# Attention scores in two pairs of PSUM banks, one exponential over each pair

## What is computed

```python
q = _conv(query, Wq[idx], 'SAME').reshape(n, HEADS, HC, -1)
k = _conv(token, Wk[idx], 'VALID').reshape(n, HEADS, HC, -1)
v = _conv(token, Wv[idx], 'VALID').reshape(n, HEADS, HC, -1)
w = jax.nn.softmax(jnp.einsum('nhcq,nhcd->nhqd', q, k), axis=-1)
a = jnp.einsum('nhcd,nhqd->nhcq', v, w).reshape(n, CA, hh, ww)
```

## Time and profile before

| what | us |
|---|---|
| median of 3 runs | 377.89 |
| lowest and highest | 376.87, 380.81 |
| the profiled execution, its time | 378.51 |
| its span, first to last instruction | 376.5 |

### The profile page before, as it was taken

One profiled execution on the slowest core, in us unless ns is written; L12 is line 12 of the kernel. 1 busy time (PEld: TensorE's weight loads), 2 busy tenths in 40 slices (PEclk: granted clock), 3 DMA queues, 4 the chain that ended last, 5 costly groups with the idle time before them and its releaser, 6 DMA issues.

```text
span 376.5 us, 5797 instructions
## 1 busy us (share of the span) xinstructions
PE 317.9 (84%) x2186; PEld 109.5 (29%) x2186; DVE 230.0 (61%) x494; ACT 173.3 (46%) x334; POOL 38.9 (10%) x36
## 2 busy tenths in 40 slices
PE   5499655688998553999999999999999899885994
PEld 1133111232343111323332323323333222332931
DVE  5970054744836650468778687878776321579944
ACT  2100000002416443987879787897978787300000
POOL 5000600400000000001010000101010012505100
PEclk9989968999989865999999999999999999999798
DMA  2799995000157953230210303000000000000001
GB/s 85 163 196 211 190 200 162 0 3 0 38 166 147 124 109 125 84 113 2 60 55 1 113 3 113 2 1 3 0 1 2 1 3 0 2 0 1 3 2 56
DMA packets 6867, 23.89 MB, mean 63 GB/s; under 512 B 1272, under 2 KB 2040, under 8 KB 5912
## 3 DMA queue, kind: packets, MB, share of 16 engines
q1 hardware_dynamic: 6840, 23.53, 26.0%
HBM read 11.59 MB, written 2.37 MB: 37 GB/s over the span
## 4 chain that ended last, share of the span: by engine, by line
PE 48%; DVE 9%; issue 4%; ACT 2%; DVEq 0%; ACTq 0%
PE ps L1179 14%; PE ps L1161 14%; PE ps L1138 11%; DVE arena_a L463 3%; PE ps L1291 2%; ACT arena_b L678 2%; PE ps L1184 2%; PE ps L1234 1%; PE ps L1251 1%; DVE arena_a L966 1%; PE ps L1007 1%; PE ps L1299 1%; DVE arena_b L978 1%; DVE arena_a L990 1%; PE ps L1242 1%
## 5 line engine op out<-in xcount | busy, mean ns | idle before, releaser
L678 ACT ACTIVATE arena_b<-ps 128x512 f32<-128x512 f32 x232 | 125.2, 607 | 37.6 <-PE ps L1161 36.9
L1161 PE MATMUL ps<-arena_a 128*128 128x512 bf16 x224 | 85.0, 389 | 10.1 <-issue 9.5
L1138 PE MATMUL ps<-arena_a 128*128 128x450 bf16 x256 | 87.4, 371 | 6.5 <-issue 4.3
L890 DVE TENSOR_REDUCE mx<-ps 128x1 f32<-128x450 f32 x120 | 69.3, 618 | 6.5 <-PE ps L1138 4.8
L885 DVE CUSTOM_DVE_ANT_0 sums<-ps,relus 128x450 bf16<-128x450 f32 x68 | 41.4, 626 | 44.3 <-PE ps L1138 34.9
L1179 PE MATMUL ps<-arena_b,vt 128*32 128x512 f32 x448 | 59.7, 605 | 0.7 <-ACT arena_b L678 0.7
L1161 PEld LDWEIGHTS ps<-arena_a 128*128 128x128 bf16 x224 | 21.7, 98 | 80.6 <-ACT arena_b L678 50.4
L686 ACT ACTIVATE relus<-ps 128x450 f32<-128x450 f32 x68 | 37.5, 554 | 10.5 <-PE ps L1138 10.4
L1007 PE MATMUL ps<-zeros 128*128 128x512 bf16 x115 | 30.4, 406 | 7.7 <-DMA xa<-x 3.5
L1138 PEld LDWEIGHTS ps<-arena_a 128*128 128x128 bf16 x256 | 24.0, 100 | 39.9 <-issue 11.3
L640 ACT ACTIVATE arena_b<-ps 96x386 f32<-96x386 f32 x3 | 1.5, 490 | 63.9 <-PE ps L1056 63.8
(11 more groups left out here) (130 smaller groups left out, 244.2 us busy)
## 6 DMA issues: line engine op xcount, KB each, us to landing
arena_b<-arena_a SPq DMA_DIRECT2D x12, 578.0 KB, 10.3
arena_b<-wmodes SPq DMA_DIRECT2D x4, 1024.0 KB, 4.9
arena_a<-k_scratch SPq DMA_DIRECT2D x3, 516.8 KB
arena_b<-arena_a SPq DMA_DIRECT2D x4, 306.0 KB, 5.7
arena_a<-q_scratch SPq DMA_DIRECT2D x3, 384.0 KB
arena_b<-arena_a SPq DMA_DIRECT2D x4, 272.0 KB, 5.0
k_scratch<-arena_b SPq DMA_DIRECT2D x3, 344.5 KB, 3.7
cst<-consts SPq DMA_DIRECT2D x1, 1029.0 KB, 11.7
```

Source lines behind the costliest of these rows:

```text
L678: nc.scalar.activation(probs[:, n % PRING, :], ps[:, SCORE_RING[n % len(SCORE_RING)], :], ACT.Exp).then_inc(expd, 1)
L890: nc.vector.tensor_reduce(mx[:, a, e:e + 1], bank, AX.X, ALU.max).then_inc(max_read, 1)
L1138: mm(ps[:, block_bank(i), 0:KHALF], qst[:, e, g, qt * P:(qt + 1) * P], kst[:, g, at:at + KHALF], start=True, stop=True).then_inc(max_score ...
L1161: last = mm(ps[:, bank, :], kst[:, g, t * P:(t + 1) * P], qst[:, e, g, :], start=True, stop=True)
```

## The change

The eight banks are dealt out anew: banks 0 and 1, and 2 and 3, are two pairs for scores, banks 4, 5 and 6 are for max blocks, bank 7 is the only one for output sums. A full step now has two groups instead of four tiles: a group is the score tiles of two heads, in the two banks of a pair, and ScalarE takes one exponential of 1024 columns over both. The last keys still make one tile of 512 columns. A half so has 15 groups (`EXP_GROUPS`) and the whole attention 112 exponentials of 1024 and 8 of 512 columns. Group n waits for the exponential of group n-2. The ring of probabilities is the same memory as four slots of 1024.

The plan keeps its 4.15 blocks a step, but hands them out after each group, and `values` moves behind the second group and its blocks. The first `values` of every half but the first waits until the output sums of the half before have been transposed. The gates and output banks are renumbered, the prologue's max blocks run over seven banks instead of six, and one `keep_clock` uses bank 3 instead of 6.

```diff
-EXP_UNITS = HEADS * DT + 1
+EXP_GROUPS = 2 * DT + 1
 PRING = 8
+GROUP_SLOTS = PRING // 2
-SCORE_RING = (0, 1, 2)
-MAX_RING = (3, 4, 5)
-O_RING = (6, 7)
+SCORE_RING = (0, 2)
+MAX_RING = (4, 5, 6)
+O_BANK = 7
@@ attention_plan
         for t in range(DT + 1):
-            units = HEADS if t < DT else 1
+            units = 2 if t < DT else 1
             due += BLOCKS_PER_STEP * (1.0 if t < DT else 0.6)
             taken = 0
             for h in range(units):
-                plan.append(("score", s * EXP_UNITS + t * HEADS + h))
+                plan.append(("score", s * EXP_GROUPS + 2 * t + h))
                 k = int(due * (h + 1) / units + 1e-6)
                 take(k - taken)
                 taken = max(taken, k)
-                if prev and h == min(2, units - 1):
+                if prev and h == units - 1:
                     plan.append(("values", *prev))
@@ block_bank
-            ring = SCORE_RING + MAX_RING if i < prologue else MAX_RING
-            return ring[i % len(ring)]
+            return i % 7 if i < prologue else MAX_RING[i % len(MAX_RING)]
@@ ScalarE
+                    width = HALF if n % EXP_GROUPS == 2 * DT else 2 * HALF
+                    at = 2 * HALF * (n % GROUP_SLOTS)
                     act.wait_ge(scored, n + 1)
-                    if n >= PRING:
-                        old_half, old = divmod(n - PRING, EXP_UNITS)
-                        act.wait_ge(pv_done, old_half * (DT + 1) + old // HEADS + 1)
-                    nc.scalar.activation(probs[:, n % PRING, :], ps[:, SCORE_RING[n % len(SCORE_RING)], :], ACT.Exp).then_inc(expd, 1)
+                    if n >= GROUP_SLOTS:
+                        old_half, old = divmod(n - GROUP_SLOTS, EXP_GROUPS)
+                        act.wait_ge(pv_done, old_half * (DT + 1) + old // 2 + 1)
+                    nc.scalar.activation(probs_row[:, at:at + width], banks(SCORE_RING[n % 2])[:, 0:width], ACT.Exp
+                                         ).then_inc(expd, 1)
@@ score_tile
-                if n >= len(SCORE_RING):
-                    pe.wait_ge(expd, n - len(SCORE_RING) + 1)
+                if n >= 2:
+                    pe.wait_ge(expd, n - 1)
-                    t, h = divmod(i, HEADS)
-                    g = b * HEADS + h
-                    last = mm(ps[:, bank, :], kst[:, g, t * P:(t + 1) * P], qst[:, e, g, :],
-                              start=True, stop=True)
+                    t, pair = divmod(i, 2)
+                    for k in range(2):
+                        g = b * HEADS + 2 * pair + k
+                        last = mm(ps[:, bank + k, :], kst[:, g, t * P:(t + 1) * P], qst[:, e, g, :],
+                                  start=True, stop=True)
@@ values
-                if t == 0 and half >= len(O_RING):
-                    pe.wait_ge(o_read, half - len(O_RING) + 1)
+                if t == 0 and half >= 1:
+                    pe.wait_ge(o_read, half)
-                    pe.wait_ge(expd, n0 + HEADS)
+                    pe.wait_ge(expd, n0 + 2)
```

## The result

The changed kernel takes 390.28 us in the median (389.22 to 391.45, four runs) against 378.07 beside it, a ratio of 1.0313 (95% interval 1.0249 to 1.0378): 3.1% slower. The forecast was 391 us.

A forecast was written before the change was run, and what follows sets the result against it. TensorE was taken to bound the kernel; stalls of +2.5, +7.9, +2, +3.5 and +0.7, less 2.1 and 1.5, made +13.0 us, so 391 us on the 377.9 median. The range ran from 381 to 399.

The forecast's parts named there:

- TensorE's saturation: In steps with blocks, TensorE gives the pace: 2.73 us a step with nothing in it but work.
- The faster rival: Waits of scores for exponentials are real time that fewer handshakes would save, giving 372 us; chance 0.10.
- Block 1 plain: Steps whose first max block is a plain maximum: block 4 stalls 0.07 us, some 36 steps, +2.5 us.
- Block 1 a diff block: Relu queues behind the wide exponential, so block 4 stalls 0.71 us; 11 steps, +7.9 us.
- Fifth block: Five full steps have one more block, which needs block 2's bank: about 0.4 us each, +2 us.
- VectorE's transposes: Transposing a half's sums and back delays block 4 about 0.3 us, twice in each of six halves: +3.5 us.
- case 3: A diff block second, third or fourth in a step: its bank is wanted only after the values, so no cost.
- The stalls of before: The earlier kernel's 0.30 us of stalls a half, contained in the other terms, go off: -2.1 us.
- The last turn: It already waits 1.30 us for the split of the maxima; values no longer lie ahead of it: +0.7 us.
- The end without blocks: Steps after the max blocks run out fall from 2.47 to 2.08 us; four such steps, -1.5 us.
- The single output bank: Rival: a half's first values wait for the previous half's transpose, about 1 us in seven halves, 399 us; chance 0.16.
- A gap that repeats on the engine that should be saturated: Sign of too few PSUM buffers; if the forecast holds, the repeating gap is ahead of block 4.

The follow-up runs named there:

- e2: The changed kernel with a block handed out after every score tile again, same banks and wide exponentials; 380.36 us, ratio 1.0093 to the kernel before.
- e8: The kernel before with the changed order, four max banks instead of three and one output bank instead of two; 379.93 us, ratio 1.0048.
- e1: The changed kernel, but ScalarE takes a diff block's Relu directly behind a score group ahead of that group's exponential; 381.83 us, ratio 1.0131 to the kernel before.
- e4: The kernel before with one bank of output sums instead of two, all else unchanged; 377.91 us, ratio 1.0028.
- e3: The kernel before with its banks and narrow exponentials, and only the order of the changed one; 388.74 us, ratio 1.0325.
- e5: The changed kernel with each group's exponential issued as two of 512 columns, one behind the other; 391.49 us, ratio 1.0336 to the kernel before.

## Why the prediction was right, and where its terms were not

The mechanism was right: the order of the list left 1.00 us between block 1 and block 4, and a Relu behind an exponential made that a stall of 0.72 us. The closeness of the total is in part luck, as the terms below show.

**What bounds it.** TensorE's saturation held: where e2 takes the stalls away a step is 2.73 us, and at no point less while it has four blocks. The faster rival, that the waits for exponentials were real time, falls: e8 has even more of them (45.6 us) at nearly the time of before.

**Block 1 plain: 0.07 us a step, +2.5 us.** Measured 0.08, +2.9 over the 36 steps from V 0.0 to V 6.3 that don't start with a diff block.

**Block 1 a diff block: 0.71 us, 11 steps, +7.9 us.** Measured 0.72 in the steps that have nothing else in them, but in nine steps, +6.5. This was the term that decided. The list of steps was right; that steps 0 and 1 of half 0 run at half clock, right behind the prologue, was overlooked. In e1 the way from the first score to V 0.0 is only 0.2 us shorter than in the changed kernel.

**Fifth block: about 0.4 us.** Right in kind. The fifth blocks added 0.53, 0.64 and 0.76 us to their steps, of which 0.19 is the block's own work: 0.34 to 0.57 of stall. The costliest stand behind a first diff block; here block 5 of such a step, from the timeline of the changed kernel, waits for block 2, which VectorE could only read after the Relu:

```profile
213.88 0.36 PE L1142 MATMUL ps<-arena_a 128*128 128x450 bf16 x1 [0.55 <-ACT relus L690]
213.96 0.63 DVE L889 CUSTOM_DVE_ANT_0 sums<-ps,relus 128x450 bf16<-128x450 f32 x1 [2.16 <-PE ps L1142]
...
214.65 0.36 PE L1142 MATMUL ps<-arena_a 128*128 128x450 bf16 x1 [0.40 <-DVE mx L889]
```

**VectorE's transposes: +3.5 us, right in sum and wrong in its working.** I had priced two events of 0.3 us in each of six halves. Transposing back costs nothing: the steps that hold it are 2.81 us in four of six halves. What the transpose of the sums costs is in the passage from V s.6 to the first values of the next half. Its work is 5.20 us (the shortest passage in e1 and e2 is 5.21). Less that work, 0.08 for a plain step, 0.72 for a first diff block and 0.19 for a fifth block's work, the six passages have 0.7, 0.8, 0.3, 0.0, 1.5 and 0.3 us left, 3.6 in all. This holds everything that is not counted elsewhere, a fifth block's stall among it, and no run takes the transpose out by itself. By the timelines it is cheap where nothing else is late, and nothing where both steps are held by a Relu anyhow. It is dear where a partner is late. After half 4, a Relu at 266.93 holds its partner on VectorE to 267.61, the transpose stands in front of the next read, and a block waits for 1.03 us beyond TensorE's own work:

```profile
268.17 0.71 DVE L911 STREAM_TRANSPOSE ot<-ps 128x512 f32<-128x512 f32 x1
...
269.70 0.36 PE L1142 MATMUL ps<-arena_a 128*128 128x450 bf16 x1 [1.03 <-DVE mx L894]
```

That passage took 7.05 us, 1.39 over the best, a fifth block among it. The late Relu is that of a third block, for which case 3 of the prediction has "Nothing"; in e1, where it comes earlier, the passage is 0.83 us shorter. So case 3 holds for the block's own bank and not for what stands behind its partner on VectorE.

**The stalls of before: -2.1, measured -3.4.** Counted in the same way, the kernel before has 3.4 us of stall from V 0.0 to V 6.3; over half of it lies in each half's last interval, V s.5 to V s.6, and is gone in the new order.

**The stretch with blocks in sum.** My terms (2.5 + 7.9 + 2 + 3.5 - 2.1) make +13.8 us; measured +12.4. Term by term the trace has about 2.9 + 6.5 + 2.4 + 3.6 - 3.4, and 0.4 in small delays.

**The last turn: +0.7, measured +0.8.** It waits for 2.13 us instead of the 1.30 of the earlier trace rows.

```profile
305.29 0.22 PE L1148 MATMUL ps<-ident_b,mparts 128*48 128x128 bf16 x1 [2.13 <-DVE mparts L873]
```

**The end without blocks: -1.5 us.** The size is about right, the working is not. In half 7 it is -1.24, of which 0.21 is the score that this interval has less, so -1.0; in half 6 it is about -0.3, which is the table's +0.31 with the turn's 0.8 taken out and the missing block's 0.19 put back. I had steps of 2.08 us; they are 2.27 and 2.35 against 2.40 and 2.47:

```profile
320.05 1.07 PE L1185 MATMUL ps<-arena_b,vt 128*32 128x512 f32 x8
321.05 0.60 PE L1167 MATMUL ps<-arena_a 128*128 128x512 bf16 x2
321.86 0.61 PE L1167 MATMUL ps<-arena_a 128*128 128x512 bf16 x2 [0.21 <-ACT arena_b L681]
322.40 1.06 PE L1185 MATMUL ps<-arena_b,vt 128*32 128x512 f32 x8
```

ScalarE came into this step behind by the gates' and cell's work (it runs from 319.34 to 323.64 without a pause), so it, and not TensorE's 1.95, still holds the second group. That a longer stretch would reach the rhythm I had worked out is not shown.

**The total.** The terms added up to +13.0 us. The two traces differ by 10.7, of which -1.05 is the earlier first score and no part of the change; the medians differ by 12.2. So 391 against 390.28 looks better than the sum was: its terms were 1.4 us high in the stretch with blocks, and the medians lie further apart than the traces.

**The single output bank.** As rival it had 0.16 and would have given 399 us. e4 prices it at 0.2 us a half at most, in the order of before; in the changed kernel it does not bind. The rule of the Trainium skill (Perfetto Trace Analysis, Matmuls) on rotating matmul groups through banks holds here for the max blocks, where a fourth bank takes the ratio from 1.0325 (e3) to 1.0048 (e8), and is worth next to nothing for the output sums. A gap that repeats on the engine that should be saturated, which the Trainium skill (the same page, Optimization Strategy) gives as a possible sign of too few buffers, is what the changed trace shows ahead of block 4.

## What to carry to other kernels

Where one engine is full, an order written by hand is a set of distances between each producer and the reuse of its buffer: a change that moves a long item (here 1 us of values) out of the middle of a step shortens all distances that ran across it. The merged exponentials were not what cost: with the same order and narrow ones the step still took 3.30 us (e3), and with a block after every score and wide ones it took 2.73 (e2). So when a merge comes with a new order, test the two apart, and look for what now stands behind the long item in its engine's queue and who waits for that.

Price such a change by walking the new list on the clock of one step, kind of step by kind: that gave the two main stalls within 0.01 us. Then ask of each step at which clock it runs, since two of the eleven steps were priced at full clock and ran at half. Rare events that are priced by a mean can come out right in sum and wrong one by one.

## What the runs showed of the hardware

An exponential over two adjacent PSUM banks costs what its columns cost: 1024 ns for 1024 columns against 607 mean for 512, with nothing to be seen of a price for crossing from one bank to the next. The line through the two copies of the earlier trace rows had given 1.02 us.

Behind an idle time of TensorE its granted clock can be about half. Behind the 9.5 us ahead of the first score it was 0.50 (before, 147 to 152 us). Behind the last turn's 2.1 us of waiting it was 0.50 to 0.53 for 2 to 3.5 us in the traces of e3, e5 and e8, and 1.00 in that of the changed kernel. What decides between the two is not shown.
